# Relation products of a graph kernel: once per 48 chunks over 216 columns, instead of once per 32 over 138

## The reference

```
seg  = dst * R + edge_type                      # R = 65
sums = segment_sum(x[src], seg).reshape(N, R, F_in)
cnt  = segment_sum(ones,   seg).reshape(N, R, 1)
agg  = sums / maximum(cnt, 1.0)
conv = einsum('nri,rio->no', agg, W_rel) + x @ W_root + bias
h    = conv + x @ W_res + b_res
h    = relu((h - mean(h)) * rsqrt(var(h) + EPS) * gamma + beta)   # over the nodes
out  = layernorm(x + h)                                           # over the features
```

## Time and profile before

| | |
|---|---|
| median of three runs | 2033.2 us |
| the profiled execution: first to last instruction | 2403.0 us |
| PE busy / weight loads busy | 2051.2 us / 1898.7 us |
| DVE / ACT / POOL busy | 1396.7 / 886.1 / 1485.5 us |
| mean granted TensorE clock | 0.935 of 2.4 GHz |
| loop over the chunks: first and last aggregation | 40.0 us and 2346.0 us |

### The profile page before, as it was taken

One profiled execution on the slowest core, in us unless ns is written; L12 is line 12 of the kernel. 1 busy time (PEld: TensorE's weight loads), 2 busy tenths in 40 slices (PEclk: granted clock), 3 DMA queues, 4 the chain that ended last, 5 costly groups with the idle time before them and its releaser, 6 DMA issues.

```text
span 2403.0 us, 38063 instructions
## 1 busy us (share of the span) xinstructions
PE 2051.2 (85%) x13396; PEld 1898.7 (79%) x13396; DVE 1396.7 (58%) x2444; ACT 886.1 (37%) x1651; POOL 1485.5 (62%) x1582
## 2 busy tenths in 40 slices
PE   5798888888888889889888889888988988888987
PEld 3687878878778878877888778777887877778887
DVE  7575565565556556547557457556556555645645
ACT  4333334333333333333333333333333333333333
POOL 6666666666666666666666666666666666666640
PEclk9999989899999989999989989999999989998999
DMA  8643434444443444444343444443343444343433
GB/s 273 162 90 89 96 88 91 94 90 91 94 93 88 90 96 89 90 96 90 88 97 86 91 95 91 91 96 87 89 96 89 90 92 90 88 91 88 91 69 108
DMA packets 244737, 233.86 MB, mean 97 GB/s; under 512 B 27097, under 2 KB 239491, under 8 KB 243907
## 3 DMA queue, kind: packets, MB, share of 16 engines
q0 software_dynamic: 223056, 203.79, 38.1%
q1 hardware_dynamic: 21491, 27.60, 3.7%
HBM read 218.48 MB, written 12.80 MB: 96 GB/s over the span
## 4 chain that ended last, share of the span: by engine, by line
PE 79%; issue 10%; DVE 4%; another core or an unknown queue 3%; ACT 2%; POOL 1%; DMA 1%; ACTq 0%; DVEq 0%; SPq 0%; POOLq 0%
PE tb L667 39%; PE ps L632 29%; PE ps L636 6%; PE tb L560 4%; DVE onehot L1018 2%; ACT agg L770 2%; POOL wsb L515 1%; DVE same L957 1%; DMA wsb<-in_x_dram,srcT 0%; DVE lst L1206 0%; DMA eth<-in_edge_type_dram 0%; PE tb L610 0%; DVE agg L1230 0%; PE tb L580 0%
## 5 line engine op out<-in xcount | busy, mean ns | idle before, releaser
L525 POOL DMA_INDIRECT xg<-xtab,srcT x1545 | 1458.5, 944 | 824.5 <-issue 359.5
L1018 DVE TENSOR_SCALAR onehot<-iota,segT,vT 128x456 fp32r<-128x456 f32 x1563 | 1086.7, 741 | 673.2 <-PE ps L636 423.4
L770 ACT ACTIVATE agg<-ps 128x390 f32 (+1 forms) x1563 | 842.0, 539 | 1454.7 <-PE ps L636 924.2
L667 PE MATMUL tb<-agg,wsb 128*128 128x138 f32 x6370 | 1212.4, 314 | 181.9 <-issue 140.7
L632 PE MATMUL ps<-onehot,xg 128*128 128x390 f32 (+1 forms) x3126 | 1195.2, 447 | 67.1 <-issue 55.9
L667 PEld LDWEIGHTS tb<-agg,wsb 128*128 128x128 f32 x6370 | 921.6, 202 | 219.8 <-issue 170.4
L632 PEld LDWEIGHTS ps<-onehot,xg 128*128 128x128 f32 x3126 | 626.6, 202 | 117.0 <-issue 103.6
L636 PEld LDWEIGHTS ps<-onehot,xg 128*128 128x128 f32 x3028 | 613.8, 203 | 56.8 <-issue 52.8
L636 PE MATMUL ps<-onehot,xg 128*128 128x66 f32 x3028 | 610.5, 202 | 35.9 <-issue 34.2
L957 DVE SCALAR_TENSOR_TENSOR same<-ps,rel 128x1088 bf16<-128x1088 f32 (+3 forms) x96 | 145.5, 1515 | 0.0
L560 PE MATMUL tb<-same,identb 128*128 128x512 bf16 x416 | 114.4, 400 | 26.5 <-DVE same L957 24.9
(11 more groups left out here) (133 smaller groups left out, 338.2 us busy)
## 6 DMA issues: line engine op xcount, KB each, us to landing
xg<-xtab,srcT POOLq DMA_INDIRECT x1545
xtab<-agg SPq DMA_DIRECT2D x4, 1536.0 KB
hinit<-H SPq DMA_DIRECT2D x1, 3125.0 KB
agg<-in_x_dram SPq DMA_DIRECT2D x4, 768.0 KB, 7.5
out_dram<-agg SPq DMA_DIRECT2D x6, 448.0 KB, 3.0
dsth<-in_dst_dram SPq DMA_DIRECT2D x23, 64.0 KB
eth<-in_edge_type_dram SPq DMA_DIRECT2D x23, 64.0 KB
srcr<-in_src_dram SPq DMA_DIRECT2D x12, 64.0 KB
```

Source lines behind the costliest of these rows:

```text
L525: pool.indirect_dma_start(out=xg[c % RING][:], out_offset=None, in_=xtab.bitcast(F32R), in_offset=bass.IndirectOffsetOnAxis(ap=srcT[t % 2] ...
L667: ins = nc.tensor.matmul(o, wsb[:, r * F:(r + 1) * F], pair_rhs(p, r), start=(r == 0), stop=(r == R - 1))
L770: nc.scalar.activation(agg_group(g)[:, :, bass.ds(off, n)], ps[c % NRB][:, 0:n * R].rearrange("f (n r) -> f r n", r=R), ACT.Copy).then_inc ...
L1018: nc.vector.tensor_scalar(onehot[o][:].rearrange("p (a b) -> p a b", a=3), iota3[:, :, 0:IW], segT[t % 2][:, k:k + 1], vT[t % 2][:, k:k + ...
```

## The change

- `GC` is 16 chunks instead of 32, and a group's window `WIN` is 72 nodes instead of 138, so a region holds 65 x 78 values per partition instead of 65 x 144.
- Three groups make a pass (`PG` = 3, 48 chunks). Five regions are held in `agg` (`NSLOT` = 5): passes with even numbers use regions 0, 1, 2 and those with odd numbers 3, 4, 2. `transform` multiplies a whole pass: 65 matmuls, each over the three windows, 216 columns. There are 33 passes instead of 49 groups. The last pass has 27 chunks in two groups.
- The products of a pass are spread over chunks 2 to 29 of the next pass (28 chunks); chunks 30 to 47 and 0, 1 have none. In the last pass they are spread over 23 chunks.
- The products have one bank, `tb[0]`; the sums of comparisons, the transposes and the last pass use `tb[1]`, and the waits that kept these apart go.
- `add_pass` adds three windows to `H` at chunk 42 of the next pass.
- To find the room, `RING` goes from 18 to 15 and `NOH` from 10 to 7, and small buffers move into parts of others. The part of `agg` that this adds is cleared by one more memset on POOL.
- `PE_CMP` = 70 and `DVE_CMP` = 76, the chunks at which the comparisons and their sums stand, stay.

```diff
-GC = 32
+GC = 16
+PG = 3
+NSLOT = 5
-WIN = 138
+WIN = 72
-RING = 18
-NOH = 10
+RING = 15
+NOH = 7
+DVE_ADD = 42
...
-    AGG = 1024 + (XT + 1) * 3 * F
+    AGG = NSLOT * PREG
...
+    def slot_of(g):
+        q, j = g // PG, g % PG
+        if j == PG - 1:
+            return PG - 1
+        return j if q % 2 == 0 else PG + j
...
-            base = (g % 2) * PREG
+            base = slot_of(g) * PREG
...
+            nc.gpsimd.memset(last, 0.0).then_inc(consts, 1)
...
                 if j == 0 and t >= 1:
-                    pe.wait_ge(h_add, pair_of_count(t) - 1)
+                    pe.wait_ge(offs_rdy, t)
...
-            def transform(p, lo, hi):
+            def pass_rhs(q, r):
+                a, m = first_slot(q) * PREG, pass_groups(q)
+                return agg[:, a:a + m * PREG].rearrange("f (s r n) -> f r s n", s=m, r=R)[:, r, :, 0:WIN]
+
+            def transform(q, lo, hi):
                 if lo == 0:
-                    pe.wait_ge(evac, min((p + 1) * GC, NCH))
+                    pe.wait_ge(evac, min((q + 1) * PC, NCH))
...
-                        pe.wait_ge(h_add, p - 1)
+                    if 1 <= q < NPASS - 1:
+                        pe.wait_ge(h_add, PG * q)
...
-                if p >= 1 and i >= 2:
-                    n = pair_len(p) - 2
-                    lo, hi = R * (i - 2) // n, R * (i - 1) // n
-                    if hi > lo:
-                        transform(p - 1, lo, hi)
+                n = min(2 * GC, pass_len(q)) - 4
+                if q >= 1 and 2 <= i < n + 2:
+                    transform(q - 1, R * (i - 2) // n, R * (i - 1) // n)
...
-                if c % GC == 0 and p >= 2:
-                    act.wait_ge(trans_ps, p - 1)
+                if c % PC == 0 and q >= 2:
+                    act.wait_ge(trans_ps, q - 1)
+                if c % PC == (PG - 1) * GC and q >= 1:
+                    act.wait_ge(trans_ps, q)
...
-                if p >= 2 and i == 6:
-                    add_group(p - 2)
+                if q >= 1 and i == DVE_ADD:
+                    add_pass(q - 1)
```

More of the change, by code:

```diff
@@ L65, in gnn @@
     GLAST = ceil_div(NR, GC)
-    assert NTL >= 2 and NPAIR >= 3 and 0 < ELAST < P
+    assert NTL >= 2 and NPASS >= 3 and 0 < ELAST < P
     W6 = SLOTS * R
@@ L178, in gnn @@
         XN1 = XN0 + (XT + 1) * F
[L179 removed]
+        XR0 = (NSLOT - 1) * PREG
+        XR1 = XR0 + 512 + 3 * F
+        assert XS0 + 3 * XPIECE * 2 * F >= PREG and XS0 + 4 * XPIECE * 2 * F >= 2 * PREG and XN0 >= 2 * PREG
+        assert XN1 + 512 <= XR0 and XR1 <= AGG
         pieces = agg[:, XS0:XN0].rearrange("p (t f) -> p t f", f=2 * F)
@@ L182, in gnn @@
         xnat = agg[:, XN0:XN1].rearrange("p (t f) -> p t f", f=F)
-        rest = agg[:, XN1:AGG]
+        rest = agg[:, XN1:XR0]
+        last = agg[:, XR1:AGG]
         head = agg[:, 0:XS0]
+        xT = agg[:, XR0:XR0 + 512]
+        wsum = agg[:, XR0 + 512:XR0 + 512 + F]
+        wroot = agg[:, XR0 + 512 + F:XR0 + 512 + 2 * F]
+        wres = agg[:, XR0 + 512 + 2 * F:XR1]
+        tail_f32 = same[:].bitcast(F32)
+        t0, t1, t2, t3 = 6 * (N // BNC), NS * BG * 6, NS * BG * 2, NS * 4 * BG
+        bst = tail_f32[:, 0:t0].rearrange("p (c s) -> p c s", s=6)
+        lst = tail_f32[:, t0:t0 + t1].rearrange("p (b t s) -> p b t s", b=NS, s=6)
+        lmv = tail_f32[:, t0 + t1:t0 + t1 + t2].rearrange("p (b t s) -> p b t s", b=NS, s=2)
+        lrs = tail_f32[:, t0 + t1 + t2:t0 + t1 + t2 + t3].rearrange("p (b k t) -> p b k t", b=NS, k=4)
         WLO = R - RING
@@ L716, in _ @@
             pe.wait_ge(bad_rdy, 1)
-            pe.wait_ge(h_add, NPAIR - 2)
-            nc.tensor.matmul(tb[(NPAIR - 1) % 2][0:1, 0:1], col(BAD), ones[:, 0:1], start=True, stop=True).then_inc(bad_ps, 1)
+            nc.tensor.matmul(turn[0:1, 0:1], col(BAD), ones[:, 0:1], start=True, stop=True).then_inc(bad_ps, 1)
             def fast():
-                transform(NPAIR - 1, 0, R)
+                transform(NPASS - 1, 0, R)
             def general():
@@ L1031, in add_group @@
                     dve.wait_ge(hinit_out, 16)
[L1032 to L1041, removed]
+                bank = out_bank if q < NPASS - 1 else turn
+                bases = registers(brow[0:1, PG * q:PG * q + m], ENG.DVE, N - 1)
+                for j in range(m):
+                    g = PG * q + j
+                    at = (slot_of(g) - first_slot(q)) * WIN
+                    if g >= 1:
+                        dve.wait_ge(h_add, g)
+                    nc.vector.scalar_tensor_tensor(out=tmph[:], in0=iota3[:, 0, 0:WIN], scalar=lastg[:, g:g + 1],
+                                                   in1=bank[:, at:at + WIN], op0=ALU.is_le,
+                                                   op1=ALU.mult).then_inc(h_tmp, 1)
+                    dve.wait_ge(h_tmp, g + 1)
+                    h = H[:, bass.ds(bases[j], WIN)]
+                    nc.vector.scalar_tensor_tensor(out=h, in0=tmph[:], scalar=1.0 / SCALE, in1=h, op0=ALU.mult,
+                                                   op1=ALU.add).then_inc(h_add, 1)
             nc.vector.memset(flags[:, NFL:NFL + 1], 0.0)
@@ L1109, in fast @@
             def fast():
-                for g in range(NPAIR - 2, LAST_G):
-                    add_group(g)
+                add_pass(NPASS - 2)
                 dve.wait_ge(h_add, LAST_G)
                 block_stats(0, EARLY)
-                for g in range(LAST_G, G):
-                    add_group(g)
+                add_pass(NPASS - 1)
                 dve.wait_ge(h_add, G)
```

114 lines of the change are left out of this document (51 added, 63 removed).

## The result

The changed kernel takes 2266.47 us (median of four runs, 2255.96 to 2269.72), the kernel before 2033.62 us in the same set of runs. The ratio is 1.114 (95% interval 1.112 to 1.115): 233 us slower. The forecast was 2192 us, with a range of 2045 to 2265.

What follows compares the result with a forecast made beforehand. The prediction took POOL's gathers, 1.246 us per chunk, to bound the kernel before. To 2033 us it added 119 for PE's lateness beyond the ring's cover, 15 for start and end and 25 for the clock: 2192 us, range 2045 to 2265.

Steps and rivals of the forecast that it cites:

- What bounds the kernel before: POOL's gathers, 1.246 us apart, set the 2033 us; PE's line is 1874; 370 us between span and median are unexplained idle.
- The wait at the comparisons: With seven one-hot buffers PE waits 2.46 us at each sum; a pair of chunks takes 4.51 us, 5.35 with products.
- rival A: POOL stays the bound, the ring covers PE's waits; only start and end remain, 2048 us; chance 0.12.
- the signs that were named: Profile after: PE's waits at sums 150 us or more, POOL's waits for PE above 459, span about 2500.
- Products: On PE, 216-column records take 0.180 us, all products 764 us against 733; a chunk with products costs 1.43 us.
- Start and end: Three gathers behind the table 3.7 us, PE ending some 10 late, last pass 0.7, one more window 0.8: 15 us.
- The clock: PE at half clock in the 40 pairs with new waits and no products: 0 to 68 us, 25 taken.
- the account of lateness: PE's lateness behind POOL over three tiles; fifteen gather buffers cover 14 us, the excess stalls POOL: 119 us in all.
- DVE's additions: Three more additions of windows per pass on DVE, lying in free chunks; uncovered they cost 34 us at most.
- B: PE's unexplained idle time is real without the profiler and no longer hidden once PE is the bound: 2259 us; chance 0.10.
- C: Faster: a fixed cost of 0.025 us per product record is saved by fewer, larger records: 1998 us; chance 0.08.

Runs made afterwards that it cites:

- before_skip_again: Kernel before without the gathers of three of its 18 ring places, so part of the computation is left out: 1846.66 us against 2033.43.
- ring15: Kernel before with RING 15 instead of 18 alone: 2038.55 us against 2034.50.
- noh7_pe73: Kernel before with NOH 7 instead of 10 and PE_CMP 73 instead of 70: 2034.66 us against 2033.43.
- cmp73_again: Changed kernel with DVE_CMP 73 instead of 76: 2057.69 us against 2034.50 for before; as cmp73, in the disturbed set, 2438.78 against 2437.24.
- noh7_again: Kernel before with NOH 7 instead of 10 alone: 2123.71 us against 2033.43; as noh7, in the disturbed set, 2650.76 against 2437.24.
- filler: Changed kernel with six unneeded matmuls of 128 columns ahead of each of the 96 waits for a comparison: 2229.55 us against the changed kernel's 2264.03.
- cmp73_skip_again: Changed kernel with DVE_CMP 73, without gathers of three of 15 ring places (part of computation left out): 1988.31 us; before 2033.43, before_skip_again 1846.66.

## Why the prediction was right, and where it was short

The direction, the cause and the place of the loss were forecast; 159 us of loss were forecast and 233 came. The time lies at the very end of the range of 2045 to 2265 us: 1.5 us above it as it stands, and at 2264 if the ratio is applied to the 2033.2 us from which the forecast started. That the result was measured in the undisturbed condition was luck, as the sum had no term for the other one.

**What bounds the kernel before: right.** The claim rested on one line that fitted the median within 4.7 us, against a profile that showed PE behind. before_skip_again (-187 us with PE's work whole) and the waits of ring15 and noh7_pe73 show it. The second half of the claim, that the 370 us of unexplained idle time belong to the profiler, was wrong: a time of 2437 us comes in runs without a profile too. And the 297.5 + 161.7 us that POOL "waited for PE" in the earlier trace rows were read too large: they hold the ordinary 0.30 us 389 times, 117 us, and the 161.7 stand under "remote", which names no engine.

**The wait at the comparisons: right in mechanism and size.** 2.43 us from chunk to sum against 2.46; pairs of 5.46 against 5.35; 189.9 us of waits, where the terms of rival A gave 15.4 a tile, 185. Taken away by one number in either design (cmp73_again, noh7_pe73) and made by one number (noh7_again). Two of the signs that were named did not come: POOL's waits for PE are 418 us and not above 459, and the span is 2268 and not about 2500. Both were set against the disturbed profile.

**Products: right.** 1.43 us a chunk, with the two small errors named above; fewer records gained nothing.

**Start and end: right where they can be seen.** ring15 +4.05 against 3.7. In cmp73_again the final products last 16.20 us, 0.67 more than the earlier trace rows, forecast 0.7:

```profile
2000.73 16.20 PE tb L685 x130
```

Between cmp73_again and ring15, spans of 2056.2 and 2037.4 us, lie 18.8 us. The last gather starts 9.2 us later (1985.9 and 1976.7), the last chunk follows it by 8.9 us more (12.7 and 3.8; forecast some 10), 0.7 are products. The 9.2 us are gathers held up in the loop; that term was missing from the 2048.

**The clock and the account of lateness: too small, together by 75 us.** The term that was mis-sized is "I take 25": 65 us were found where it stands, 41 of which filler shows to be the clock. From its 70th to its 86th chunk a tile takes, in the profile after:

| comparisons begin at chunk of the pass | forecast without clock | measured, mean of four | of it at half clock |
|---|---|---|---|
| 22 (4 pairs with products) | 39.4 us | 45.8 us | 12 to 20 us |
| 6 (8 pairs with products) | 42.8 us | 41.6 us | 0 |
| 38 (2 pairs with products) | 37.8 us | 48.8 us | 27 to 34 us |

Forecasts are 8 pairs of 4.51 or 5.35 us. The differences add to 16.2 us per three tiles, 65 us in all, where I took 25 out of 0 to 68: the pairs without products ran at half clock for most of their length. The rest of the three tiles took 397.3 us against the 388.3 of the account (3 x 159.5 + 29.8 - 120.0), 36 us in all; another 10 to 27 us per tile ran at half clock there. 40 and 36 make up the 76 us between 2192 and the 2268.0 of the profile. That the first 40 are mostly the clock is shown by the two tables; the other 36 were not separated from DVE's additions and ACT's pace.

The forecast tied the half clock to the new waits alone. It comes without them too: cmp73_again, with 34.7 us of waits left, has a mean granted clock of 0.950, which is 206 us at half clock, and some 95 of these lie in chunks that have neither products nor comparisons. The old products, spread over nearly all chunks, have 0.994 in ring15 (26 us, all at the start and end). At POOL's pace this costs little; where PE is the pace, as in the changed kernel, it counts.

The rivals: A (the ring covers it) was refuted by the result: POOL's gaps beyond 0.30 us add to 230 us, and the time of A, 2048, is about what comes without the waits (cmp73_again, 2057.69). B (idle time without the profiler) didn't occur in the undisturbed runs but is real in the disturbed ones, where noh7 lost 214 us and cmp73 nothing. C was refuted by cmp73_skip_again.

What stays open: what PE waits for in the disturbed condition. In cmp73's profile of it the idle time stands under "issue" as it does in the earlier trace rows:

```profile
PE ps L656 <- issue: 105.5, 87, 4.0
```

No experiment was made on it. It is no fixed property of a chip: the disturbed set and the last undisturbed one ran on the same chip. And no version beat both kernels: noh7_pe73 equals before with three buffers fewer.

## What to carry to other kernels

Where two engines hand work to each other at fixed places in their orders, the room is the lead that the buffers allow less the distance between the places; when a buffer count is lowered, go through every such pair. When the gain sought is fewer instructions on an engine, first see whether the engine's time goes by instructions or by columns, and whether it is the pace at all: here it went by columns, and the pace was POOL's. A loss on one engine is made good only as far as that engine has room in the rest of the loop, so look at the room too before work is bunched. A periodic wait also has a second price, the clock of what follows it: bound it by all the work in the stretch with the waits, not by a third of it; here the bound was 68 us, 25 were taken and 65 were found.

## What the runs showed of the hardware

- A gather of 128 rows of 1 KB took 1.24 us on POOL at the least: 0.94 us and 0.30 between two. Its 0.94 us are the same in both conditions (median 0.937 us in cmp73, 0.939 in ring15). The idle time without a releaser in the disturbed profiles stands on PE, ACT and DVE (in cmp73 142, 110 and 44 us).
- The kernel before took 2033 and 2437 us in different sets of runs, each set within 0.4% of itself, and one chip showed both. Its order relative to others changed with it: cmp73 is 1.1% slower in one condition and equal in the other.
- PE was granted half its clock for 20.5 us in which it was busy for 14.98, with no single wait above 2.4 us.
- Matmuls without use, placed inside a wait, gave back 34 us.
